# A decoder layer with attention, an S4D convolution and an expert stage: the convolution's transforms on folded halves, and new step lists

## The chip, the cores and the metric

The kernel runs on one core of one Trainium2 chip. Its time is the device time of an execution in microseconds (us); the number compared is the median of the runs. The engines are TensorE (PE; its weight loads are shown as PEld), VectorE (DVE), ScalarE (ACT), GpSimd (POOL) and SyncE (SP), which issues most of the DMAs.

## The reference

Input x is (4, 512, 128) in fp32; everything is fp32 with a norm behind each of three sublayers.

```python
x = layernorm(x + attention(x))        # 16 heads of 8, 4 kv heads, rms norm, rope, tanh cap 50, causal
x = layernorm(x + xattn(x, ctx_768))   # below
x = layernorm(x + ffn(x))              # 2 shared experts + top 2 of 8, hidden 512

def s4d(x):                            # inside xattn
    K  = 2 * real(einsum('dn,dnl->dl', dC, exp(dtA[:, :, None] * arange(L))))
    Kf = rfft(K, n=2 * L);  xf = rfft(x, n=2 * L, axis=1)
    return irfft(xf * Kf.T, n=2 * L, axis=1)[:, :L] + x * D_skip
# xattn: c = top-32 cross attention over 32 context rows; x = layernorm(x) * (1 + g*scale_in(c)) + g*shift_in(c)
#        y = s4d(x) * (1 + g*scale_out(c)) + g*shift_out(c); xt = x_text + y
#        xt = xt + gelu(layernorm(xt) @ W1 + b1) @ W2 + b2; return layernorm(xt)
```

## The kernel before

Every engine plays a list of steps written out in full (`PE_ORDER`, `ACT_ORDER`, `POOL_ORDER`, `DVE_ORDER`, played by `play`). A step name is followed by its numbers: `s.1.3.4` is batch 1, head pair 3, score fill 4. The order on an engine is exactly that of its list, and the engines meet at semaphores. SyncE has its own program, which issues loads and stores in order.

**Attention.** For each of 4 batches: `xT`, `qkv`, rms norm and rope (`squares`, `rms`, `rope`, `parts`, `copies`), `qT` (queries and keys transposed, six banks evacuated by ScalarE and VectorE in turn), then for 8 head pairs six score fills `s` into two PSUM banks `ring_s`; ScalarE evacuates each with tanh and then does one `exp` per pair; POOL masks; TensorE multiplies by the values (`PV`, one per two pairs), VectorE copies (`oT`). `probs` holds three pairs. Then `rows`, `yT`, `proj`, `x1`.

**The S4D kernel.** While batch 0 and the start of batch 1 run, VectorE, ScalarE and POOL compute exponentials and angles in four parts (`steps`, `states`, `pack`, then `angles`, `turns`, `exponents`, `powers`, `products`, `amounts` with .0 to .3), TensorE multiplies them (`taps`), VectorE writes `kij` (`evacuate`), which goes out to DRAM and comes back as `kld` (`load_kernel`). `first_tap` adds the skip. `kernel.0` to `kernel.7` transform it with the tables `cosm` and `sin_fwd`, and `spectra` scales the result into `kc`, `ks`, `kcn`.

**The convolution.** Per batch, xn is normed and modulated (`film`, `modulate`); `dft.b.0` to `.7` multiply xn (four tiles of 128 tokens) with `cosm` and `sin_fwd` (512 x 512, four row tiles) into `ring_u`; `spectrum` multiplies by the kernel's spectrum; `conv.b.0` to `.7` multiply back with `cosm` and `sin_inv` into `bank_d`; `shape_out` follows, then a feed-forward (`h`, `hT`, `up`, `gelu`, `down`, `ffT`, `ff_norm`, `x2_norm`, `x2`). Each of dft and conv has 8 x 4 products of 128 x 128 by 128 x 128.

**Start of the program.** `functions` (two sines and a tanh for the S4D states) and `fold1` to `fold4` (the cross attention's weights multiplied together) run at the head of the lists; `vf.b` on VectorE evacuates `fold4`.

**Experts.** `x2T`, `gates`, `route`, `weights`, `rank`, `place` per batch; for each group of two batches `rows.g` on VectorE builds the table of blocks (`table_ready`) and the row numbers (`rows_ready`). POOL scatters the tokens to DRAM (`scatter.b.j`, two issues each, 16 issues a group). SyncE waits for the scatters, loads the rows back in six loads (`load_rows`, `x_blk`) and then one 514 KB block of expert weights for each of 23 blocks of 128 rows (`load_block`, six slots). The units are numbered 0 to 77: 0 to 15 shared experts of batches 0 and 1, 16 to 38 the blocks of group 0, 39 to 54 shared experts of batches 2 and 3, 55 to 77 the blocks of group 1. A unit has `blk_up`, `blk_gelu` and `blk_down`; a block also has `blkT` (transpose of its rows, `xT_blk` with `RING` slots, copied by VectorE), `weigh` (VectorE, into `y_blk` with `YS` slots) and `blk_out` (POOL sends it to DRAM by indirect DMA). At the end SyncE loads the pairs back (`load_pair`), VectorE adds and norms (`pairs`, `out_begin`, `out_end`) and SyncE stores.

A y slot is free when its send has landed:

```python
def weigh(s):
    dve.wait_ge(u_down, s + 1)
    if k >= YS:
        dve.wait_ge(y_sent[k % YS], 16 * (k // YS))
```

## Time and profile before

| what | us |
|---|---|
| median of 3 runs (558.0 to 561.37) | 561.07 |
| the profiled execution | 563.88 |
| its span, first to last instruction | 562.1 |
| busy: TensorE / VectorE / ScalarE / POOL | 443.5 / 330.3 / 328.2 / 247.3 |
| granted TensorE clock, mean of the span | 0.904 |

The busy time of an engine is the sum of its instructions. A matmul is pipelined with the next, so the time of one is longer than the distance between two; the distance is what a stretch of them costs. The granted clock of 1.00 is 2.4 GHz, 0.50 is 1.2 GHz. "[2.28 <-DVE y_blk L1838]" behind a row says that the engine was idle for 2.28 us before it, until that instruction of VectorE released it. Terms of the plan are told from the profiled execution, whose span is 1.0 us above the median.

### The profile page before, as it was taken

The page shows a single profiled execution, that of the slowest core. Times are in us where ns is not written, and L with a number is a line of the kernel's source. Part 1 is how long each engine was busy: PE and PEld are TensorE (multiplying, and loading weights), DVE is VectorE, ACT ScalarE, POOL GpSimd, SP SyncE. Part 2 cuts the span into 40 slices and gives each one's busy share as a digit, 9 for nine tenths or more (in the row PEclk, how much of TensorE's full clock was granted, in tenths as well). Part 3 has the DMA queues.
Part 4 walks back from the last instruction along what each step waited for, and adds up shares of the span by engine and source line. Part 5 has one row for each costly group of instructions (what it writes and reads, how often), then busy time and mean ns, then how long its engine had stood idle before and what let it go on. Part 6 is the DMA issues. An engine that isn't in the chain of part 4 may idle for free.

```text
span 562.1 us, 9639 instructions
## 1 busy us (share of the span) xinstructions
PE 443.5 (79%) x3343; PEld 316.1 (56%) x3361; DVE 330.3 (59%) x983; ACT 328.2 (58%) x567; POOL 247.3 (44%) x306
## 2 busy tenths in 40 slices
PE   4656667378988879788798999999979699989830
PEld 3322323145657633567346865787778666878830
DVE  7877968847876565866754775546245310334214
ACT  4279769997775888877896152215536343445410
POOL 3513264423561565614446244864283574044341
PEclk9856656679999999999999999999998899999985
DMA  3788300002101000000000200165485516769831
GB/s 94 267 181 152 100 2 1 0 2 58 77 1 77 20 2 0 2 1 1 2 0 1 76 2 19 40 179 194 138 260 160 163 54 182 261 208 279 271 104 37
DMA packets 39920, 51.53 MB, mean 92 GB/s; under 512 B 8769, under 2 KB 29025, under 8 KB 39873
## 3 DMA queue, kind: packets, MB, share of 16 engines
q1 hardware_dynamic: 37376, 45.78, 28.1%
q0 software_dynamic: 2496, 5.15, 2.6%
q8 instruction: 27, 0.44, 0.3%
q14 instruction: 21, 0.16, 0.1%
HBM read 41.25 MB, written 13.86 MB: 98 GB/s over the span
## 4 chain that ended last, share of the span: by engine, by line
PE 47%; ACT 22%; DVE 9%; issue 8%; POOL 8%; DMA 5%; another core or an unknown queue 1%; POOLq 0%; SPq 0%; ACTq 0%; DVEq 0%
ACT probs L1082 8%; PE ring_s L957 5%; ACT probs L1088 5%; PE bank_o L987 4%; PE bank_o L775 4%; PE bank_d L865 3%; DMA token_pairs<-y_blk,x_blk 3%; PE ring_s L760 3%; PE bank_o L973 3%; PE ring_s L951 3%; POOL expert_rows L1302 3%; PE ring_u L852 3%; PE bank_d L894 2%; PE ring_u L844 2%; PE bank_r L641 2%
## 5 line engine op out<-in xcount | busy, mean ns | idle before, releaser
L1082 ACT ACTIVATE probs<-ring_s 128x512 f32<-128x512 f32 (+1 forms) x192 | 92.3, 524 | 39.2 <-PE ring_s L760 19.5
L760 PE MATMUL ring_s<-qT,kT 128*128 128x128 bf16 (+3 forms) x238 | 62.5, 330 | 41.6 <-ACT probs L1082 31.3
L1254 POOL TENSOR_SCALAR_AFFINE_SELECT probs<-probs 128x256 f32<-128x256 f32 (+1 forms) x96 | 50.6, 558 | 100.1 <-ACT probs L1088 100.1
L1135 ACT ACTIVATE g_ring<-ring_s,w_blk 128x128 f32<-128x128 f32 x184 | 52.3, 371 | 47.5 <-PE ring_s L957 47.5
L1088 ACT ACTIVATE probs<-probs 128x2560 f32<-128x2560 f32 x32 | 74.4, 2335 | 1.1
L1311 POOL DMA_INDIRECT token_pairs<-y_blk,x_blk x46 | 44.6, 970 | 66.2 <-DVE y_blk L1838 59.9
L760 PEld LDWEIGHTS ring_s<-qT,kT 128*128 128x128 bf16 x256 | 20.8, 100 | 80.2 <-ACT probs L1082 61.0
L957 PE MATMUL ring_s<-xT_blk,w_blk 128*128 128x128 f32 x368 | 51.1, 284 | 5.9 <-DVE xT_blk L1831 3.9
L1188 POOL TENSOR_TENSOR rstd<-var_eps,neg_half 128x4 f32<-128x4 f32 x24 | 25.0, 1040 | 67.4 <-DVE var_eps L1507 67.4
L957 PEld LDWEIGHTS ring_s<-xT_blk,w_blk 128*128 128x128 f32 x368 | 46.5, 198 | 7.9 <-ACT g_ring L1135 4.3
L775 PE MATMUL bank_o<-probs,vv 128*32 128x128 f32 (+3 forms) x512 | 43.2, 483 | 3.7 <-POOL probs L1254 3.6
L1131 ACT ACTIVATE g_ring<-ring_s,vcols 128x512 f32<-128x512 f32 x32 | 21.7, 687 | 40.8 <-PE ring_s L951 40.8
L987 PE MATMUL bank_o<-w_blk,g_ring 128*128 128x128 f32 x280 | 40.2, 290 | 4.1 <-DVE y_blk L1838 4.1
L1302 POOL DMA_INDIRECT expert_rows<-x_rows,rows_i x32 | 31.6, 989 | 20.5 <-DVE gmax L1823 11.6
L987 PEld LDWEIGHTS bank_o<-w_blk,g_ring 128*128 128x128 f32 x280 | 36.5, 203 | 6.1 <-issue 5.6
L973 PEld LDWEIGHTS bank_o<-w_sh,g_ring 128*128 128x128 f32 x256 | 32.9, 192 | 11.7 <-issue 11.7
L973 PE MATMUL bank_o<-w_sh,g_ring 128*128 128x128 f32 x256 | 33.8, 275 | 0.0
L951 PE MATMUL ring_s<-x2T,w_sh 128*128 128x512 f32 x64 | 32.8, 597 | 0.3 <-ACT g_ring L1131 0.3
L775 PEld LDWEIGHTS bank_o<-probs,vv 128*32 128x32 f32 x512 | 16.0, 119 | 30.2 <-issue 22.3
L1831 DVE COPY xT_blk<-bank_m 128x128 f32<-128x128 f32 x35 | 10.1, 287 | 34.0 <-PE bank_m L641 33.8
L1838 DVE TENSOR_SCALAR y_blk<-bank_o,x_blk 128x128 f32<-128x128 f32 x35 | 12.2, 348 | 27.8 <-PE bank_o L987 21.4
L747 PE MATMUL ring_s<-identb,qs 128*128 128x128 bf16 x128 | 11.8, 260 | 7.9 <-issue 3.5
(365 smaller groups left out, 932.3 us busy)
## 6 DMA issues: line engine op xcount, KB each, us to landing
w_blk<-expert_pack SPq DMA_DIRECT2D x46, 514.0 KB, 5.0
expert_pack<-in_L_ffn_W SPq DMA_DIRECT2D x16, 256.0 KB, 8.9
expert_rows<-blank SPq DMA_DIRECT2D x6, 520.0 KB, 3.6
x_blk<-expert_rows SPq DMA_DIRECT2D x10, 260.0 KB, 4.4
y_pair<-token_pairs SPq DMA_DIRECT2D x4, 512.0 KB, 4.9
x_in<-in_x SPq DMA_DIRECT2D x4, 256.0 KB, 2.9
cosm<-in_c_cos SPq DMA_DIRECT2D x1, 1024.0 KB, 5.9
sin_fwd<-in_c_sin_fwd SPq DMA_DIRECT2D x1, 1024.0 KB, 8.8
```

Of the source, the lines that this page charges most:

```text
L760: last = mm(bank[:, c:c + w], kT[:, r, p // 2, P * j:P * (j + 1)], qT[:, p, P * j:SEQ], start=True, stop=True)
L775: last = mm(bank_o[32 * h:32 * h + 32, P * j:SEQ], vv[:, j, q, :], probs[:, (2 * quad + h // 2) % PAIRS_HELD, c:c + SEQ - P * j], start=(j ...
L951: last = mm(bank[:, :], w_sh[:, e, P * n:P * (n + 1)], x2T[:, of, :], start=True, stop=True)
L957: last = mm(bank[:, P * n:P * (n + 1)], w_blk[:, k % SLOTS, P * n:P * (n + 1)], xT_blk[:, k % RING, :], start=True, stop=True)
L973: last = mm(bank_o[:, P * j:P * (j + 1)], g[:, P * j:P * (j + 1)], w_sh[:, e, HID + P * n:HID + P * (n + 1)], start=(c == 0 and j == 0), s ...
L987: last = mm(dst, g[:, P * n:P * (n + 1)], w_blk[:, k % SLOTS, HID + HC + P * n:HID + HC + P * (n + 1)], start=(n == 0), stop=(n == HC - 1))
L1082: f(probs[:, pair % PAIRS_HELD, BASE[n]:BASE[n] + WIDTH[n]], ring_s[k % 2][:, 0:WIDTH[n]], ACT.Tanh, scale=1.0 / (CAP * float(np.sqrt(np.f ...
L1088: f(probs[:, (b * NPAIR + p) % PAIRS_HELD, :], probs[:, (b * NPAIR + p) % PAIRS_HELD, :], ACT.Exp, scale=CAP).then_inc(exp_done, 1)
L1135: last = f(g_ring[:, s % RING, P * n:P * (n + 1)], ring_s[s % 2][:, P * n:P * (n + 1)], ACT.Gelu, bias=w_blk[:, k % SLOTS, HID + n:HID + n ...
L1254: last = g.affine_select(out=v, in_=v, compare_op=ALU.is_ge, fill=0.0, base=0, pattern=[[0, v.shape[1]], [1, P]], channel_multiplier=-1)
L1302: g.indirect_dma_start(out=rows_dram, out_offset=bass.IndirectOffsetOnAxis(ap=rows_i[:, k, j:j + 1], axis=0), in_=x_rows[:, k, j, :], in_o ...
L1311: g.indirect_dma_start(out=pair_dram, out_offset=bass.IndirectOffsetOnAxis(ap=x_blk[:, k % NB, D:D + 1].bitcast(I32), axis=0), in_=y_blk[: ...
```

## The change

Three things change together.

**Folded transforms.** The frequencies are moved by half a sample, so that the transforms of the even and of the odd half of a folded sequence need tables of half the size. `halves` (26 small VectorE instructions by Newton steps on 128 x 4 values) computes the cosines and sines of the half step, `half.0` to `.3` turn the loaded tables by it, and `tab.0` to `.3` transpose them on TensorE for the forward direction (ScalarE copies them out). The tables loaded are `cos_inv` and `sin_inv`, four loads of 256 KB, instead of three of 1 MB. `flip` is a matrix that turns a tile over, made by three POOL operations. `mirror` (two products with it) and `fold` (VectorE, two operations on 128 x 256) make sums and differences of xn and its mirror image; `dft` and `conv` then have 8 x 2 products each; `unfold` (three operations), `back` (two products) and `shape_out` in two parts undo it. The kernel goes the same way (`kmirror`, `kfold`, `kernel`), and `spectra` turns its spectrum by the half step.

**Experts.** `RING` goes from 3 to 4 and `YS` from 3 to 6. SyncE requests the first six weight blocks of a group as soon as `table_ready` comes, ahead of its wait for the scatters; for group 1 it also waits for the sent blocks of group 0 and loads the first pair of batches before that wait. The load of x for batch 2 goes ahead of the kernel's way through DRAM.

**Lists.** All four lists are written anew, with the new steps in them. `taps` uses `ring_u` instead of `bank_d` and `bank_r`.

```diff
-RING = 3
+RING = 4
 SLOTS = 6
-YS = 3
+YS = 6
@@ PE_ORDER, the start (before, then after)
-    xT.0 qkv.0 fold1 fold2 fold3 fold4 vectors qT.0.0 qT.0.1 qT.0.2 qT.0.3 qT.0.4 s.0.0.0 s.0.0.1 s.0.0.2 s.0.0.3
+    xT.0 qkv.0 qT.0.0 qT.0.1 qT.0.2 fold1 qT.0.3 qT.0.4 qT.0.5 fold2 fold3 fold4 s.0.0.0 s.0.0.1 s.0.0.2 s.0.0.3
...
+    s.0.2.4 s.0.2.5 s.0.3.0 PV.0 s.0.3.1 s.0.3.2 xT.1 s.0.3.3 s.0.3.4 s.0.3.5 rows.0 qkv.1 PV.1 taps.0 s.0.4.0
...
@@ PE_ORDER, around gates.3 (before, then after)
-    blk_down.26 blkT.30 blk_up.29 x2T.3 blk_down.27 blkT.31 gates.3 blk_up.30 blk_down.28 blkT.32 blk_up.31
+    blk_down.24 hT.3 blkT.28 blk_up.27 up.3.0 up.3.1 up.3.2 up.3.3 down.3.0 down.3.1 down.3.2 down.3.3 blk_down.25
+    blk_up.35 x2T.3 blk_down.33 blkT.37 blk_up.36 blk_down.34 blkT.38 gates.3 blk_up.37 blk_down.35 blk_up.38
+    blk_down.36 rank.3 blk_up.39 blk_down.37 blk_up.40 blk_down.38 blk_up.41 blk_down.39 blk_up.42 blk_down.40
...
+    blk_up.53 blk_down.51 blkT.55 blk_up.54 blk_down.52 blkT.56 blk_up.55 blk_down.53 blkT.57 blk_up.56 blk_down.54
@@ ACT_ORDER, the start (before, then after)
-    xT.0 qkv.0 functions fold1 fold2 fold3 qT.0.0 qT.0.2 qT.0.4 s.0.0.0 s.0.0.1 s.0.0.2 s.0.0.3 s.0.0.4 s.0.0.5
+    xT.0 qkv.0 qT.0.0 qT.0.2 functions fold1 fold2 fold3 qT.0.4 s.0.0.0 s.0.0.1 s.0.0.2 s.0.0.3 s.0.0.4 s.0.0.5
@@ POOL_ORDER, the scatters (after)
+    mask.3.6 mask.3.7 root copies.1 root root shape_out.2 copies.0 root h.2 xn.3 scatter.1.0 scatter.1.1 scatter.1.2
+    blk_out.34 blk_out.35 blk_out.36 scatter.3.0 blk_out.37 blk_out.38 scatter.3.1 scatter.3.2 scatter.3.3
@@ DVE_ORDER, the start (before, then after) and around rows.1 (after)
-    steps squares.0 rms.0 rope.0 parts.0 v.0 copies.0 vectors vf.0 qT.0.1 vf.1 qT.0.3 states pack angles.0 turns.0
+    steps squares.0 rms.0 rope.0 parts.0 copies.0 halves qT.0.1 qT.0.3 half.0 half.1 vf.0 vf.1 qT.0.5 v.0 states pack
+    vectors angles.0 turns.0 oT.0 vf.2 vf.3 half.2 half.3 products.0 amounts.0 angles.1 evacuate.0 turns.1 tokens.0
+    gates.3 route.3 weigh.35 weights.3 weigh.36 place.3 rows.1 weigh.37 weigh.38 settle.46 blkT.55 blkT.56 blkT.57
@@ SyncE
+            for m, k in ((cos_inv, "c_cos"), (sin_inv, "c_sin_inv")):
+                rows = t[k].rearrange("(h p two) f -> two p h f", h=NJ, two=2)
+                for odd in range(2):
+                    load(m[:, NJ * odd:NJ * (odd + 1), :], rows[odd][:, :, 0:HALF], ld_dft)
...
             for g in range(GROUPS):
                 sp.wait_ge(table_ready, g + 1)
+                for q in range(SLOTS):
+                    load_block(g * NB + q)
+                if g:
+                    sent(g - 1)
+                    load_pair(GB * (g - 1))
                 sp.wait_ge(scattered[g], 16 * 2 * NT * GB)
                 for n in range(x_loads):
                     load_rows(g, n)
+                if g:
+                    load_pair(GB * g - 1)
+                for q in range(SLOTS, NB):
@@ TensorE
+            def turn_over(dst, src, at):
+                for j in range(NJ):
+                    last = mm(dst[:, P * j:P * (j + 1)], flip[:, :], src[:, at + NJ - 1 - j, :], start=True, stop=True)
+                return last
+            def half_dft(f, c, src):
+                at = 0 if (f == 0) == (c < NJ) else NJ
+                for j in range(NJ):
+                    last = mm(ring_u[f][:, P * c:P * (c + 1)], (cos_fwd, sin_fwd)[f][:, j, P * c:P * (c + 1)], src[:, at + j, :],
+                              start=(j == 0), stop=(j == NJ - 1))
+                return last
             def dft(b, n):
                 f, c = divmod(n, NT)
                 if n == 0:
-                    pe.wait_ge(xmod_ready, b + 1)
-                mat = (cosm, sin_fwd)[f]
-                for j in range(NT):
-                    last = mm(ring_u[f][:, P * c:P * (c + 1)], mat[:, j, P * c:P * (c + 1)], xn[:, j, :],
-                              start=(j == 0), stop=(j == NT - 1))
+                    pe.wait_ge(fold_ready, b + 1)
+                last = half_dft(f, c, xn)
...
@@ VectorE
+            def half(c):
+                then()
+                if c:
+                    dve.wait_ge(half_ready, c)
+                co, si = cos_inv[:, c, :], sin_inv[:, c, :]
+                op(ts(turned[0][:, :], si, sin_b[:, c:c + 1], None, ALU.mult))
+                one(ts(turned[1][:, :], co, sin_b[:, c:c + 1], None, ALU.mult))
+                op(stt(out=co, in0=co, scalar=cos_b[:, c:c + 1], in1=turned[0][:, :], op0=ALU.mult, op1=ALU.subtract))
+                stt(out=si, in0=si, scalar=cos_b[:, c:c + 1], in1=turned[1][:, :], op0=ALU.mult, op1=ALU.add).then_inc(half_ready, 1)
+            def fold_over(x, ps):
+                one(tt(x[:, NJ:NT, :], x[:, 0:NJ, :], ps, ALU.subtract))
+                return tt(x[:, 0:NJ, :], x[:, 0:NJ, :], ps, ALU.add)
...
```

## Rows read from the trace of the kernel before

**Rows 1.** Stages: busy us (x) of PE, PEld, DVE, ACT, POOL; clock, DMA.

```profile
33.70:111.80 78.10, 46.45 (x361) 20.76 (x364) 63.53 (x120) 66.27 (x87) 31.77 (x39) 0.61 0.35 71
111.80:174.60 62.80, 53.65 (x547) 35.72 (x551) 43.94 (x115) 50.99 (x70) 25.40 (x40) 0.94 0.13 42
174.60:246.30 71.70, 61.28 (x489) 38.93 (x496) 49.95 (x143) 55.50 (x76) 34.90 (x46) 1.00 0.03 10
246.30:311.00 64.70, 55.01 (x425) 35.61 (x426) 40.30 (x117) 48.97 (x68) 28.10 (x39) 1.00 0.00 1
311.00:378.00 67.00, 65.50 (x425) 49.49 (x414) 40.75 (x148) 19.48 (x28) 35.05 (x33) 1.00 0.20 58
...
482.70:539.40 56.70, 50.29 (x421) 47.27 (x420) 21.09 (x77) 27.05 (x94) 22.59 (x24) 1.00 0.70 225
```

**Rows 2.** TensorE's groups by line: records, busy us, mean ns, idle before.

```profile
L865 PE MATMUL bank_d<-spec,cosm 128*128 128x128 f32 x128 | 17.2, 278 | 0.1
...
L852 PE MATMUL ring_u<-xn,cosm 128*128 128x128 f32 x128 | 16.9, 279 | 0.1
...
L705 PE MATMUL ring_u<-pv,cosm 128*128 128x128 f32 x32 | 4.1, 275 | 0.1
```

**Rows 3.** The chain in order of time: start us, us, what.

```profile
187.63 3.57 PE bank_d L865 x32
```

**Rows 4.** VectorE's groups by line and shape, three widths.

```profile
L1838 DVE TENSOR_SCALAR y_blk<-bank_o,x_blk 128x128 f32<-128x128 f32 x35 | 12.2, 348 | 27.8 <-PE bank_o L987 21.4 <-DMA token_pairs<-y_blk,x_blk 6.4
...
L1507 DVE TENSOR_SCALAR var_eps<-mean_var 128x4 f32<-128x4 f32 x24 | 4.1, 171 | 0.8
...
L1703 DVE TENSOR_TENSOR spec<-spec,fb 128x512 f32<-128x512 f32 x4 | 2.8, 692 | 0.1
```

**Rows 5.** Timeline of ScalarE, 9 to 27: start us, us, instruction, [idle before].

```profile
9.21 1.28 ACT L1006 ACT_TABLE_LOAD   x1
...
26.39 1.02 ACT L1071 ACTIVATE qT<-ring_s 128x1024 bf16<-128x1024 bf16 x1 [8.53 <-PE ring_s L747]
```

**Rows 6.** Timelines of SyncE and VectorE, 16 to 26.

```profile
16.52 0.51 SPq L503 DMA_DIRECT2D sin_inv<-in_c_sin_inv  x1
...
24.75 0.43 DVE L1590 COPY k_parts<-k_parts 128x1024 bf16<-128x1024 bf16 x1
```

**Rows 7.** DMA issues by line: count, KB each, median us to landing.

```profile
x_blk<-expert_rows SPq DMA_DIRECT2D x10, 260.0 KB, 4.4
...
sin_inv<-in_c_sin_inv SPq DMA_DIRECT2D x1, 1024.0 KB, 10.8
```

**Rows 8.** Timelines of POOL, SyncE, TensorE at group 0's rows.

```profile
345.17 1.23 POOL L1302 DMA_INDIRECT expert_rows<-x_rows,rows_i  x1 [6.52 <-DVE gmax L1823]
...
370.93 3.29 SPq L503 DMA_DIRECT2D x_blk<-expert_rows  x6
...
378.01 0.27 PE L641 MATMUL bank_m<-ident,x_blk 128*128 128x128 f32 x1
```

**Rows 9.** Timelines of VectorE and TensorE at a y slot's wait.

```profile
419.99 0.35 DVE L1838 TENSOR_SCALAR y_blk<-bank_o,x_blk 128x128 f32<-128x128 f32 x1 [2.40 <-DMA token_pairs<-y_blk,x_blk]
...
420.49 2.05 PE L987 MATMUL bank_o<-w_blk,g_ring 128*128 128x128 f32 x8 [2.28 <-DVE y_blk L1838]
```

**Rows 10.** Timelines of TensorE, POOL, SyncE from hT.3 to group 1.

```profile
391.20 0.60 PE L641 MATMUL bank_r<-ident,fa 128*128 128x128 f32 x4
...
426.85 0.96 PE L913 MATMUL bank_r<-router_w,x2T 128*128 128x8 f32 x8
...
439.62 0.96 POOL L1302 DMA_INDIRECT expert_rows<-x_rows,rows_i  x1 [5.06 <-DVE gmax L1823]
...
469.92 0.96 POOL L1302 DMA_INDIRECT expert_rows<-x_rows,rows_i  x1 [0.30 <-issue]
...
472.73 3.23 SPq L503 DMA_DIRECT2D x_blk<-expert_rows  x6
...
482.75 0.27 PE L641 MATMUL bank_m<-ident,x_blk 128*128 128x128 f32 x1
```

399 lines of the change are left out of this document (240 added, 159 removed).

## The prediction

> **What bounds the kernel now.** I read the page's busy shares, then the busy time of each engine stage by stage, then the timelines of the places where an engine waits. The attention of the four batches ends near 311 us, the expert stage near 539, and 23 us of output follow. In batch 0 (33.7 to 111.8) ScalarE is busy 66.3 of 78.1 us and VectorE 63.5, because VectorE also builds the S4D kernel; TensorE has the lower clock there (0.61 granted), but is busy only 46 us. In batches 1 to 3 TensorE is the fullest engine, 53.7 of 62.8, 61.3 of 71.7 and 55.0 of 64.7 us, with ScalarE at 51.0, 55.5 and 49.0. From 311 to 378 TensorE is busy 65.5 of 67.0 [rows 1]. Later it is dense except for a few stalls. So a vector microsecond is dear before 112, a tensor microsecond is worth part of itself in batches 1 to 3, and nearly all of itself behind 311.
>
> **The transforms.** The fp32 product is two records: a batch has 64 products in `dft` and `conv` and the trace 128 records (L852 and L865 have 256 each, of which one of the two like groups stands here, and L705 64) [rows 2]. 32 records follow each other in 3.57 us, 0.112 us each [rows 3]. After the change a batch has 2 + 16 + 16 + 2 = 36 products, 72 records. It saves 56 x 0.112 = 6.3 us per batch. The S4D kernel's transform goes from 64 records to 36, -3.1 us, and the 16 transposes of `table` (one record each) add 1.8 us, up to 4 at the lower clock. In all 576 records become 324 + 16: 26 us less for TensorE. By place: batch 1 has half of a batch's transforms, the kernel's and 8 transposes: -3.1 - 3.1 + 1.1 = -5.1. Batches 2 and 3 have a batch's worth each, -6.3. Behind 311 lie conv.2, dft.3 and conv.3: -3.1 - 6.3 = -9.4.
>
> How much of the 17.7 us in batches 1 to 3 shortens them? TensorE is busy 85% of the time and ScalarE 77 to 81%, so another engine comes next soon. Bounds: nothing, and all 17.7. I take somewhat over half, **-10 us**.
>
> **What VectorE gets.** `halves` is 26 instructions on 128 x 4 elements. The row of that width is 171 ns, and with the hand-over by semaphore I take 0.2: 5.0 us. For the 256-wide operations the trace has no row; the bounds are 0.35 (128 x 128) and 0.69 (128 x 512) [rows 4]; I take 0.4. `half` x4 is 16 of them, 6.4 us; `fold`, `unfold` and the split `shape_out` add 2.3 us per batch. `spectra` becomes 16 instructions of 128 x 128 and a copy for 3 of 0.69: +4 us. In batches 1 to 3 VectorE has 35% free, so I cost these at nothing; without that cover they are 3 to 7 us per batch. In batch 0 it has 14.6 us free in 78, and 11 us are added.
>
> **The start.** The new lists put `halves` ahead of qT.0.1 and move `functions`, fold1, fold2 and fold3 on ScalarE behind qT.0.2, though ScalarE did all that from 9.2 to 17.9 and then was idle 8.5 us until the first transposed queries at 26.4 [rows 5]. The copies before it end near 25.1 [rows 6]; `halves` ends at 30.1 and qT.0.1 leaves its bank at 30.8. ScalarE does qT.0.2 by 29.6, then 3.3 us of functions and 0.6 us of fold1. TensorE has fold2 behind qT.0.5 (34), and its chain through kbd, wvf, xq and fold4 is most of that 8.7 us stretch of ScalarE's, 8 us, so to 42; qT.0.5 waits on VectorE for vf.0 and vf.1, which wait for fold4, and leaves its bank near 43. The first tanh of the scores opened the stage at 33.7 and comes near 42 to 43: **+9 us**. Behind it `states`, `pack`, `angles` and `turns` shift by 13, and taps.0 now stands ahead of s.0.4.0, so that scores wait for products. The new lists also mix tanh and exp of batch 0 anew, which can win some back. I take **+10 us** at the start of batch 1; bounds +3 (the lists win back most) and +22 (none won back, the 11 added vector microseconds all on the path). The tables must have landed by 25.1: three megabytes went out and the last, issued at 16.5, landed 10.8 us later, at 27.3 [rows 6, 7]; now one megabyte in four parts goes out, and at that pace it is there by 22. Flip's three small POOL operations stand ahead of the masks that fold1 needs, and fold1 now has time until 28: nothing. Four table copies on ScalarE are 0.6 us each: in the +10.
>
> So attention ends at 311 + 10 - 10 = 311.
>
> **The first expert group.** The rows of group 0 were loaded at 370.9 and TensorE took the first at 378.0 [rows 8]. TensorE's work now brings it there 9.4 us sooner, 368.6. POOL issues one scatter in 1.26 us (25 issues from 439.6 to 469.9 [rows 10]). The 16 of group 0 began at 345.2 [rows 8] and were mixed with norms; in the new list they stand together, 20.2 us, and 1.9 us (469.9 + 1.0 to 472.7) to the load makes 367.3, landing 4.4 us later at 371.7 (the median of such a load [rows 7]). So I take 371.8: -6.2. Six weight blocks are requested at `table_ready`, ahead of the scatters. Without that the weights would land 5 to 6 us behind the rows and eat most of the -6.2; they are what lets it stand. Then YS 3 to 6 removes a wait: VectorE stood 2.4 us for a sent y slot at 417.6 to 420.0, TensorE behind it 2.3 us, and then it ran at the lower clock: from 420.5 to 426.9 it did 30 records, 3.4 us at their spacing, in 6.4, so 3.0 are lost: -5.3 in all [rows 9, 10].  A stall on VectorE's `rows.1`, which stood ahead of row copies, goes too: the new list has all 23 row copies before it. It lies behind gates.3, where the chain counts, and is worth nothing in the sum.
>
> **The hand-over to group 1.** This is where that gain is given back. gates.3 moves from behind blk_up.30 to behind blkT.38, six units (12 us) later in TensorE's order; its data come by way of hT.3, ffT.3 and x2.3. A unit is 17 records, 1.9 us, so hT.3, now behind blk_up.26, is at 371.8 + 12 x 1.9 + 1.2 = 396 (391.2 before), and from there to gates.3 went 35.7 us with the 5.3 of stall in them, so it runs near 428 (426.9 before) [rows 10]. From it: 12.8 us to the first scatter (as before), 18 POOL issues at 1.26 us (16 scatters and blk_out.37 and .38; before they were mixed with nine) 22.7, 1.9 to the load, 4.4 to landing: 42, so blkT.55 near 470. TensorE has only 17 units and two biases, 31 us, ahead of it and stands about 11 us, near 459 to 470. Before: 482.75. That is **-12.7 us** for everything from 311 to blkT.55. The early weights count here as well: before, they were requested behind the six row loads, which take 3.2 us to issue [rows 10]; in that order they would add 4 to 5 us.
>
> **Group 1 and the end.** From 482.7 to 539.4 TensorE was busy 50.3 of 56.7 [rows 1]. The stalls there (y slots, row copies, one wait for a root on POOL) go in half by RING and YS: -3, and 1 us back since it starts at the lower clock: -2. The last sends no longer queue behind a blocked y copy: one issue, -1.3.
>
> **Sum.** +10 - 10 - 12.7 - 2 - 1.3 = -16 on the profiled span of 562.1: 546. That execution took 563.9 us with what lies around the span, the median of the three runs is 561.1; I take the median as the span less 1: **545 us**.
>
> **Rivals.** (a) VectorE becomes the bound of batch 0. For: 63.5 of 78.1 busy, 11 added, with `halves` ahead of everything and `rms.1`, `parts.1` behind the angles. Against: 14.6 us are free. Its price is the upper bound, +22 at batch 1, and with VectorE late the tensor saving of batch 1 is lost too (-5 instead of -10). The tail is counted from the end of attention, so 562 + 22 - 5 - 16 = 563, less 1, and with no gain in group 1 about 566; at +28 it is over 1% slower, near 570. It decides from a shift of batch 1 by 19 us. Chance 0.17, of which 0.1 slower.
> (b) Tensor time in batches 1 to 3 is not the bound (ScalarE's 51 to 56 us and its waits are). Then -10 becomes -2, 553. For: ScalarE and TensorE wait for each other in turn at two score banks. Chance 0.2.
> (c) The hand-over is longer than 42 us (POOL shares with blk_outs, gates.3 comes later than 428): 10 us more, 555 to 556. For: in the trace POOL and VectorE are in order and POOL's norms are on the way to x2.3. Chance 0.13.
> (d) The clock. In batch 0 the granted clock was 0.61 at 59% busy, in batch 1 0.94 at 85%, then 1.00 [rows 1]: the level of 1.2 GHz goes with waits between products. With 6 us less work per batch, batches 1 to 3 are 77% busy, and the 11 us stand before blkT.55 is a gap of a kind that at 417 to 420 did bring the lower level. If a third of each batch runs at it, some 15 us of products take twice their time, half of it on the path: +8 per batch, 545 + 24 = 569. Chance 0.08. The Trainium skill, "TensorE: Matmul & The Clock Gate", section "HAM oscillation — how this bites in real kernels", says that idle gaps between products send the engine back to the lower rate and each burst then starts cold. By that rule taking work away speaks against this change; the trace agrees at 420.5, and batches 2 and 3 at 1.00 with waits in them speak against its reaching so far.
> (e) The new order wins the whole front back and the stall at 459 is half: 545 - 7 - 5 = 533. Chance 0.1.
>
> My own forecast (540 to 551) has 0.32. The range: 532 to 567 leaves out part of (a), (d) and (e). Within 1% is 555.5 to 566.7, about what a measurement can tell from no change. Faster by over 1%: 0.32 + 0.2 + 0.07 of (c) + 0.1 = 0.69. Same: 0.07 of (a), 0.06 of (c), 0.02 of (d): 0.15. Slower: 0.16.
>
> **What would show it.** First tanh of the scores at 42 to 43, batch 1 near 121 (111 before). Records of L705, L852 and L865's successors 324 and no more. Attention's end (last PV) near 311; TensorE busy 78% in batches 2 and 3. First x_blk transpose near 372, gates.3 near 428, a TensorE stall of about 11 us ahead of blkT.55, named as row loads. No VectorE wait for sent y slots. I am wrong if batch 1 starts beyond 130, if batches 1 to 3 are as long as before, or if the stall ahead of blkT.55 is over 20 us.

## The result, and the profile after

| | before | after | forecast |
|---|---|---|---|
| median, us (5 runs each) | 560.73 (558.0 to 561.37) | 570.85 (568.43 to 574.2) | 545 |
| ratio to before | 1 | 1.0191 [1.0145, 1.0237] | |
| span of the profiled execution | 562.1 | 572.4 | 546 |
| first tanh of the scores | 33.7 | 43.0 | 42 to 43 |
| first tanh of batches 1, 2, 3 | 110.5, 180.7, 246.3 | 127.5, 198.1, 270.1 | batch 1 near 121 |
| last product with the values (end of attention) | 311.3 | 334.8 | 311 |
| first `x_blk` transpose | 378.0 | 397.3 | 371.8 |
| gates.3 | 426.8 | 454.4 | 428 |
| blkT.55 | 482.7 | 493.6 | 470 |
| last `weigh` | 539.0 | 549.7 | |

The rows behind the ratio are read from the profiled executions, of which that of the kernel after was the longest of its five (574.2 us). Ratios and their 95% intervals leave out executions more than 1.5% above the fastest of their kernel.

The changed kernel is 1.9% slower. Two more comparisons, each on another chip, gave 1.0237 [1.0186, 1.0288] and 1.0198 [1.0143, 1.0254]. The whole loss is there at the end of attention: +23.5 us where I forecast 0. From there to blkT.55 it wins 12.7 us (171.5 before, 158.8 after; I forecast -12.7), and behind that 0.5.

The table of busy time by stage of the kernel after, with the cuts of [rows 1] as far as they go (us from and to, length; busy us and records of PE, PEld, DVE, ACT, POOL; granted clock, DMA share, GB/s):

```profile
33.70:111.80 78.10, 48.16 (x284) 19.72 (x283) 57.09 (x132) 59.21 (x81) 33.36 (x45) 0.68 0.29 57
111.80:174.60 62.80, 43.22 (x469) 24.77 (x466) 45.49 (x110) 50.45 (x71) 22.13 (x30) 0.77 0.10 31
174.60:246.30 71.70, 56.48 (x392) 32.47 (x393) 49.10 (x134) 51.41 (x71) 29.31 (x41) 0.95 0.05 19
246.30:311.00 64.70, 52.09 (x403) 30.33 (x402) 44.49 (x140) 51.74 (x72) 28.47 (x38) 0.97 0.01 1
```

Beside [rows 1] the first stage holds less work: ScalarE 59.2 us for 66.3, VectorE 57.1 for 63.5, TensorE 284 records for 361. The work has not grown there, it comes later. TensorE did get less to do:

```profile
L915 PE MATMUL bank_d<-spec,cos_inv 128*128 128x128 f32 x64 | 10.0, 278 | 0.1
L739 PE MATMUL ring_u<-xn,cos_fwd 128*128 128x128 f32 x64 | 8.1, 277 | 0.1
L733 PE MATMUL ring_u<-xn,flip 128*128 128x128 f32 x16 | 2.6, 284 | 0.0
```

These are three of TensorE's groups by line. L865 and L852 had 128 records each [rows 2]. With the like groups (`sin_inv`, `sin_fwd`, the kernel's and the flips of `bank_d`) there are 324, as forecast, and 16 transposes of tables. The saving was there. What it was worth is the question of the experiments.

### The profile page after: what moved, and what is told of

Same layout as the page of the kernel before. It is cut to its first block, busy times and chain, and to the rows that moved or that the text cites. A ratio compares the mean times of both kernels' runs of the same rounds, so it can differ in the third digit from the quotient of the medians.

```text
span 572.4 us, 9281 instructions
## 1 busy us (share of the span) xinstructions
PE 428.2 (75%) x3125; PEld 288.0 (50%) x3125; DVE 347.5 (61%) x1065; ACT 332.2 (58%) x571; POOL 249.3 (44%) x309
## 4 chain that ended last, share of the span: by engine, by line
PE 43%; ACT 20%; DVE 13%; issue 10%; POOL 8%; DMA 4%; POOLq 0%; SPq 0%; ACTq 0%; DVEq 0%
ACT probs L1141 8%; PE ring_s L1011 6%; PE bank_o L823 5%; ACT probs L1147 4%; PE ring_s L808 3%; PE bank_o L1041 3%; PE ring_u L892 2%; PE bank_o L1027 2%; POOL expert_rows L1361 2%; POOL probs L1313 2%; DMA token_pairs<-y_blk,x_blk 2%; PE bank_d L915 2%; PE bank_m L662 2%; PE bank_d L948 2%; PE ring_s L1005 2%
## 5 line engine op out<-in xcount | busy, mean ns | idle before, releaser
L808 PE MATMUL ring_s<-qT,kT 128*128 128x512 bf16 (+3 forms) x256 | 69.5, 339 | 40.7 <-ACT probs L1141 31.8
L808 PEld LDWEIGHTS ring_s<-qT,kT 128*128 128x128 bf16 x256 | 21.4, 102 | 84.2 <-ACT probs L1141 68.3
L823 PE MATMUL bank_o<-probs,vv 128*32 128x128 f32 (+3 forms) x512 | 47.2, 519 | 6.7 <-POOL probs L1313 6.7
L1011 PE MATMUL ring_s<-xT_blk,w_blk 128*128 128x128 f32 x368 | 49.3, 277 | 3.0 <-DVE xT_blk L1968 1.7
L1011 PEld LDWEIGHTS ring_s<-xT_blk,w_blk 128*128 128x128 f32 x368 | 44.8, 192 | 4.7 <-ACT g_ring L1194 4.0
L1041 PE MATMUL bank_o<-w_blk,g_ring 128*128 128x128 f32 x280 | 38.0, 279 | 5.9 <-DVE y_blk L1975 5.9
L1027 PEld LDWEIGHTS bank_o<-w_sh,g_ring 128*128 128x128 f32 x256 | 33.1, 192 | 12.7 <-issue 12.7
L1041 PEld LDWEIGHTS bank_o<-w_blk,g_ring 128*128 128x128 f32 x280 | 34.2, 192 | 8.3 <-issue 6.7
L823 PEld LDWEIGHTS bank_o<-probs,vv 128*32 128x32 f32 x512 | 17.3, 125 | 35.8 <-issue 25.1
L795 PEld LDWEIGHTS ring_s<-identb,qs 128*128 128x128 bf16 x128 | 9.5, 114 | 26.3 <-issue 19.5
```

The costliest lines, as they stand in the source:

```text
L808: last = mm(bank[:, c:c + w], kT[:, r, p // 2, P * j:P * (j + 1)], qT[:, p, P * j:SEQ], start=True, stop=True)
L823: last = mm(bank_o[32 * h:32 * h + 32, P * j:SEQ], vv[:, j, q, :], probs[:, (2 * quad + h // 2) % PAIRS_HELD, c:c + SEQ - P * j], start=(j ...
L1011: last = mm(bank[:, P * n:P * (n + 1)], w_blk[:, k % SLOTS, P * n:P * (n + 1)], xT_blk[:, k % RING, :], start=True, stop=True)
L1027: last = mm(bank_o[:, P * j:P * (j + 1)], g[:, P * j:P * (j + 1)], w_sh[:, e, HID + P * n:HID + P * (n + 1)], start=(c == 0 and j == 0), s ...
L1041: last = mm(dst, g[:, P * n:P * (n + 1)], w_blk[:, k % SLOTS, HID + HC + P * n:HID + HC + P * (n + 1)], start=(n == 0), stop=(n == HC - 1))
```

## The experiments

Kernels measured together ran on one chip and share the runs of the kernel before there. The kernel before took 559 to 561 us on some chips and 571 to 580 on others; the last section tells what differs in the traces. So totals are compared on one chip only. Up to the end of attention the chips agree: kernels with the lists of before end it at 309.8 to 314.2 on all of them.

### Is it the head of the lists?

The first suspicion was `halves` and the late `fold` steps at the start. `a_head` is the kernel after with this part of its lists put back nearly as before, and `a_head2` is the same kernel on another chip.

```diff
 PE_ORDER
-xT.0 qkv.0 qT.0.0 qT.0.1 qT.0.2 fold1 qT.0.3 qT.0.4 qT.0.5 fold2 fold3 fold4 s.0.0.0
+xT.0 qkv.0 fold1 fold2 fold3 fold4 vectors qT.0.0 qT.0.1 qT.0.2 qT.0.3 qT.0.4 qT.0.5 s.0.0.0
 DVE_ORDER
-copies.0 halves qT.0.1 qT.0.3 half.0 half.1 vf.0 vf.1 qT.0.5 v.0 states pack vectors angles.0 turns.0
+v.0 copies.0 vectors vf.0 qT.0.1 vf.1 qT.0.3 qT.0.5 states pack angles.0 turns.0 halves half.0 half.1
```

> The changed kernel with the head of its lists put back: functions, fold1 to fold3 on ScalarE and fold1 to fold4 and vectors on TensorE stand ahead of qT.0.0 again; on VectorE the halves and half.0, half.1 go behind turns.0 and half.2, half.3 behind vf.3, and qT.0.5 stands ahead of states. Theory O (the order of the lists is what costs): the first tanh of the scores comes at 34 instead of 43, the 9 us stay to the end, and the kernel takes 562 to 565. Rival V (the added vector work makes VectorE the bound of batch 0): the first tanh comes early as well, but the 11 us of added vector work are still there, batch 1 opens no sooner than 124, and the time stays within 3 us of the changed kernel, 568 to 571. Rival C (the lower clock in batches 0 and 1 sets the pace): a gain of at most half of the 9 us, 566 to 568.

> The kernel of a_head once more, since TensorE's semaphore increments came late behind 360 us there. Theory O: the first tanh at 33, batch 1 at 117 to 120, attention's end at 321 to 326, as there; and with increments on time the total is 561 to 565.

Measured: first tanh at 32.3 and 33.7 (41.1 to 43.0 in three traces of the kernel after), but batch 1 at 119.3 and 122.4 (125.4 to 127.5), and attention ends at 325.5 and 330.4 (330.1 to 334.8). Ratios 1.0432 [1.0359, 1.0505] and 1.0458 [1.0399, 1.0517], on chips of the slower kind. Of some 9 us won at the head 3 to 8 are left at batch 1, where theory O wanted all of them to the end. The head costs what I forecast, but it is not the main cause.

### Is it VectorE's new work, or the order?

`a_nohalf` is the kernel after without the work on the half-sample tables: `halves` sets two small tiles to constants and `half` does one tiny memset, so the tables aren't turned. `a_head_nohalf` is the same with the head of `a_head`.

```diff
 def half(c):
-    co, si = cos_inv[:, c, :], sin_inv[:, c, :]
-    op(ts(turned[0][:, :], si, sin_b[:, c:c + 1], None, ALU.mult))
...
+    v.memset(turned[0][:, 0:1], 0.0).then_inc(half_ready, 1)
```

> The changed kernel without the work that makes the half-sample tables on VectorE: the 24 small instructions that find the half-angle columns and the 16 instructions of half.0 to half.3 (128 x 256) are left out, two memsets and four tiny ones stand for them (the tables are then not shifted by half a sample). All lists are as changed. Rival V (the added vector work is what lengthens the start and batch 0, 5.0 + 6.4 us by my prices): first tanh 4 us sooner, batch 1 opens at 116 to 120 instead of 126, total 561 to 565. Theory O (the order of the lists, not the work in it): first tanh and batch 1 within 2 us of the changed kernel, total 568 to 572.

> The changed kernel with the head of its lists put back as in a_head, and without the half-sample table work on VectorE as in a_nohalf (tables not shifted by half a sample). With the head put back, batch 1 opened 3 to 6 us sooner, not 9, and VectorE was busy 74 of batch 0's 88.7 us; with the table work left out but the head as changed, nothing moved. If the two stand in each other's way (the changed order hides the 10 us of table work ahead of the late first tanh, and the repaired head brings them into batch 0, where VectorE is full): first tanh at 33, batch 1 at 114 to 117, attention's end at 319 to 323. If the table work costs nothing anywhere: batch 1 at 119 to 122, attention's end at 326 to 330.

Measured: `a_nohalf` has its first tanh at 40.9 and batch 1 at 125.7, the kernel after 41.3 and 125.6 in its second execution. In the stage from the one to the other:

```profile
41.00:125.80 84.80, 51.01 (x398) 23.09 (x398) 62.96 (x138) 67.33 (x88) 33.51 (x38) 0.63 0.19 38
```

VectorE is busy 63.0 us for 65.9 and nothing is shorter. `a_head_nohalf` has 34.1 and 119.1, `a_head` and `a_head2` 32.3 and 119.3, 33.7 and 122.4. So the table work costs nothing in the changed order, and 0 to 3 us at batch 1 behind the mended head; that the two stand in each other's way, my next idea, fell (114 to 117 was forecast). The rest of the new work of VectorE (`fold`, `unfold`, `spectra`) was left out in neither.

The other half of the question is `b_neworder`: the kernel before, products and all, with the lists of the kernel after less the new steps (`tab`, `kmirror`, `mirror`, `back`, `halves`, `half`, `kfold`, `fold`, `unfold`), `RING` 4, `YS` 6 and the early weights. It ran beside `a_head`.

```diff
-RING = 3
+RING = 4
-YS = 3
+YS = 6
 PE_ORDER
-... hT.0 up.0.0 up.0.1 s.2.4.3 s.2.4.4 up.0.2 s.2.4.5 s.2.5.0 up.0.3 PV.9 s.2.5.1 down.0.0 down.0.1 down.0.2 down.0.3 s.2.5.2
+... s.2.5.3 s.2.5.4 up.0.1 up.0.2 up.0.3 film.1.0 film.1.1 film.1.2 down.0.0 down.0.1 down.0.2 s.2.5.5 s.2.6.0 s.2.6.1
...
```

> The kernel before with its own full transforms (no halves, no folds, none of the added vector work), but with the new lists in all four engines (the new steps taken out), RING 4, YS 6 and the early weights. Theory O: batch 1 opens at 124 or later, attention ends at 335 or later although no vector work was added, and with the full transforms the kernel is slower than the changed one: 575 to 590. Rival V: without the added vector work batch 1 opens at 116 or sooner, attention ends near 320 and the time is 560 to 567.

Measured: 623.54 us, 1.0924 [1.084, 1.1008]. Attention ends at 348.0; `b_loads` (below), which has the old lists and the same slots and loads, ends it at 311.3 on the same chip. Theory O is borne out, and its 575 to 590 was too low. Here are the four batches of the kernel before in a second execution, of the kernel after in a second execution, and of `b_neworder`. The cuts were set by hand near the first tanh of each batch, up to 1.5 us from it:

```profile
32.60:109.30 76.70, 46.90 (x360) 20.63 (x360) 62.37 (x118) 65.22 (x86) 31.63 (x38) 0.61 0.37 75
109.30:176.30 67.00, 58.66 (x613) 38.03 (x614) 48.30 (x123) 53.59 (x74) 26.29 (x41) 0.96 0.13 45
176.30:245.40 69.10, 59.90 (x443) 37.69 (x440) 46.65 (x138) 53.83 (x75) 34.90 (x46) 0.98 0.02 5
245.40:310.30 64.90, 56.01 (x428) 35.72 (x427) 40.46 (x120) 48.56 (x68) 28.12 (x39) 1.00 0.00 1
```

```profile
41.30:125.70 84.40, 48.79 (x398) 20.88 (x398) 65.86 (x144) 67.35 (x88) 33.54 (x38) 0.67 0.16 36
125.70:195.00 69.30, 53.15 (x511) 32.14 (x512) 53.36 (x138) 54.88 (x77) 25.98 (x39) 0.88 0.09 28
195.00:265.50 70.50, 54.34 (x365) 30.24 (x364) 45.22 (x135) 54.05 (x75) 31.95 (x42) 0.98 0.05 20
265.50:330.20 64.70, 54.55 (x408) 31.01 (x406) 45.30 (x143) 49.17 (x68) 30.96 (x44) 0.97 0.00 1
```

```profile
41.10:125.70 84.60, 46.39 (x386) 19.61 (x385) 64.05 (x133) 66.45 (x86) 32.26 (x38) 0.65 0.25 48
125.70:199.20 73.50, 60.68 (x565) 38.51 (x564) 48.51 (x120) 53.96 (x75) 26.62 (x39) 0.85 0.09 26
199.20:278.00 78.80, 63.62 (x416) 38.11 (x416) 42.92 (x135) 54.53 (x75) 33.41 (x46) 0.91 0.05 18
278.00:348.80 70.80, 62.19 (x465) 38.77 (x463) 40.60 (x125) 48.58 (x67) 28.52 (x39) 0.93 0.01 1
```

By the exact first tanh of each batch and the last product with the values the lengths are:

| | head | batch 0 | batches 1, 2, 3 | their sum |
|---|---|---|---|---|
| old order, old transforms | 32.3 | 76.6 | 68.8, 67.2, 65.0 | 201.0 |
| new order, new transforms | 41.3 | 84.4 | 69.3, 70.5, 64.6 | 204.4 |
| new order, old transforms (`b_neworder`) | 40.3 | 84.5 | 73.6, 78.7, 70.8 | 223.1 |

The order of the lists costs 8.1 at the head, 7.9 in batch 0 and 22.1 in batches 1 to 3, together 38.1 us (36.7 against `b_loads`); the smaller transforms, with all that came with them, give 18.7 of it back. The other traces of the kernel before have 200.7 for the sum, those of the kernel after 207.4 and 207.6, so what is given back is 15.5 to 18.7. ScalarE's work is the same in all three (221.2, 225.5 and 223.5 us in attention). What grew is the time in which it is not busy, by the windows above: in batches 1 to 3 45.0 us in the old order, 66.0 in the new one with the old transforms, 46.4 with the new ones; in batch 0 11.5, 18.2 and 17.1. That is nearly the whole cost of the order.

One site can be read off. In the new `PE_ORDER` nine products of 512 columns in fp32 stand between two score fills: s.2.5.4, up.0.1 to up.0.3, film.1.0 to film.1.2, down.0.0 to down.0.2, s.2.5.5. ScalarE's timeline there, first of the kernel after, then of `b_neworder` (start us, us, instruction, idle before it and who ended it):

```profile
244.27 2.82 ACT L1141 ACTIVATE probs<-ring_s 128x256 f32<-128x256 f32 x6 [5.11 <-PE ring_s L808]
```

```profile
254.63 2.82 ACT L1091 ACTIVATE probs<-ring_s 128x256 f32<-128x256 f32 x6 [5.11 <-PE ring_s L769]
```

Both stand 5.11 us until the next fill. The longest wait of ScalarE for a fill in the kernel before was 3.4 us, in its waits:

```profile
ACT probs L1082 <- PE ring_s L760: 30.2, 44, 3.4
```

The length of the run alone does not make the wait. Before, eight such products and two columns of `dft` stood between s.3.6.3 and s.3.6.4, and in the new lists ten stand between s.3.6.1 and s.3.6.2. There ScalarE had `gelu`, `exp` and `ff_out` to do meanwhile, and waited 1.45 us in the kernel before and 0.96 in `b_neworder`:

```profile
295.53 0.38 ACT L1082 ACTIVATE probs<-ring_s 128x256 f32<-128x256 f32 x1 [1.45 <-PE ring_s L760]
```

```profile
331.04 1.08 ACT L1091 ACTIVATE probs<-ring_s 128x512 f32<-128x512 f32 x2 [0.96 <-PE ring_s L769]
```

At s.2.5.5 it had nothing else. A second wait of this size is not for a fill: at attnT.1, a transpose of the cross attention that stands behind PV.9 and rows.8 on TensorE, ScalarE waits 5.06 us in `b_neworder` and 4.97 in the kernel after; before, its waits for this bank in batch 2 add up to 1.4. (The step writes the tile `x1T`.)

```profile
237.25 0.60 ACT L1112 ACTIVATE x1T<-bank_r 128x512 f32<-128x512 f32 x1 [5.06 <-PE bank_r L650]
```

No other single wait for a fill is over 3 us in the new order; the rest of the 22.1 is spread over many places, and none was tried by itself.

For batch 0 VectorE's waits from the first tanh to batch 1 tell the places (waiting line, releaser: us in total, times, longest), of the kernel before and then of the kernel after:

```profile
DVE pv L1479 <- ACT ue L1044: 2.0, 2, 1.4
```

```profile
DVE pt L1530 <- ACT pv L1093: 6.7, 1, 6.7
DVE pv L1544 <- ACT ue L1103: 4.5, 2, 2.6
DVE uf L1536 <- ACT ug L1089: 3.2, 1, 3.2
```

The S4D kernel's pieces go to and fro between ScalarE and VectorE. VectorE stood 14.4 us for them in the new order and 2.0 in the old; in `b_neworder`, without any new step, these waits are 16.6. This fits the 7.9 us, but I did not mend these places one by one, so it is a reading. What lengthens batch 0 to 85 to 89 us when the head is mended stays open.

### What is a microsecond of TensorE worth in attention?

`b_half` is the kernel before with half the products of `dft`, `conv` and `kernel`; the sums are incomplete. Nothing else moves.

```diff
-for j in range(NT):
+for j in range(NT // 2):
     last = mm(ring_u[f][:, P * c:P * (c + 1)], mat[:, j, P * c:P * (c + 1)], xn[:, j, :], ...)
```

> The kernel before with nothing changed but that dft, conv and the kernel's transform leave out every second half of their products (32 instead of 64 records' worth in each batch; the sums are then incomplete): TensorE gets what the change gives it and more (32 products fewer per batch, 7.2 us, and 3.6 once), and no engine gets any new work. It measures by itself the step that I took at -10 us for batches 1 to 3 (by its size here 7.2 + 7.2 + 7.2 = 21.6 us less, of which I would have counted 12) and the 10.8 us behind attention. Theory O (TensorE's time inside attention is worth little, since each score fill waits for ScalarE): attention ends at 303 to 308, total 550 to 556. My forecast's step: attention ends at 299 or sooner, total 545 or less. Rival C (less work brings the lower clock, which eats the gain): attention ends at 309 or later with a granted clock under 0.97 in batches 2 and 3, total 556 or more.

Measured: 559.19 for 559.46, 1.0005 [0.9964, 1.0046]. Up to the end of attention the trace has 193 transform records for 385, 21.5 us less of TensorE at the 0.112 us of [rows 3], and attention ends at 309.9 for 309.9. Its batches 1 to 3:

```profile
110.70:177.90 67.20, 55.11 (x552) 32.23 (x552) 49.67 (x127) 53.70 (x75) 25.88 (x40) 0.94 0.13 45
177.90:243.90 66.00, 54.19 (x373) 31.50 (x372) 45.09 (x134) 53.59 (x75) 34.88 (x46) 0.95 0.02 5
243.90:310.20 66.30, 53.54 (x362) 30.88 (x362) 40.45 (x122) 48.37 (x68) 29.85 (x40) 0.90 0.00 1
```

By the exact first tanhs they take 67.3 + 66.0 + 66.5 = 199.7 us, 1.3 less than before. Batch 3 with 65 fewer records is 1.5 us longer: the granted clock is 0.90 where it was 1.00, and 7.3 us less work lowered the busy time by 2.5. In batch 2 the clock took less (between its exact first tanhs 60 records, 6.7 us, went and the busy time fell by 4.6), and still only 1.3 us were won. So both theory O and rival C have a part, and every sign that I had set for rival C came true; this run cannot part them further. In the old order these products, the clock that they hold up included, are worth next to nothing.

`a_double` is the kernel after with the products of `dft` and `kernel` done twice and the conv columns filled with as many extra products, so TensorE has somewhat over the old amount of transforms in the new order (412 records in batches 1 to 3; 385 before, 220 after).

```diff
-for j in range(NJ):
+for j in [*range(NJ)] * 2:
     last = mm(ring_u[f][:, P * c:P * (c + 1)], (cos_fwd, sin_fwd)[f][:, j, P * c:P * (c + 1)], ...)
```

> The changed kernel with every product of dft and kernel issued twice and four extra products in each column of conv (results unchanged): TensorE's products are back at the number before, all else is as changed. Theory O and no part of the clock: attention gets 8 to 14 us longer (335 to 343 or more) and the kernel 15 to 25 us longer, 585 to 595. Rival C (the lower clock of batches 1 to 3 is what lost the gain): the granted clock rises from 0.77 in batch 1 and 0.95 in batch 2, attention ends at 338 or sooner and the kernel takes 575 to 583.

> The changed kernel once more, beside the others. Where the late increments are absent: 570, attention ends at 335, ratio 1.02. Where they are there: 585 to 600, since its sixteen scatters of a group stand together, with the same front.

Measured on the chip of `b_half`: `a_double` 601.08, 1.0778 [1.0702, 1.0855]; the kernel after 571.46. Attention ends at 344.4 for 330.1. Its batch 0 is 84.8 us, its batches 1 to 3 are 77.0 + 74.3 + 68.3 = 219.5, 15.1 above the 204.4 of the kernel after, for 192 records, 21.5 us. `b_neworder` has 164 records more than the kernel after in these batches, 18.4 us, and is 18.7 us longer. So the same products are worth next to nothing in the old order and most or all of their time in the new one. That this is because scores wait in line behind runs of other products fits ScalarE's idle time above; it was not tested by moving single products.

> The kernel before once more, for its trace on the same chip as the runs beside it. In the four experiments before this, semaphore increments of TensorE were seen 1 to 16 us late while POOL's indirect DMAs landed (none was late by over 1 us in the first traces of the kernel before and of the changed one), and the kernel before took 566 to 579 us there instead of 561. If that belongs to the chip, this trace shows it for all four kernels of this call or for none; attention ends at 311 in either case, since no indirect DMA runs before that.

The kernel before gave 557.88 there, with increments on time and the end of attention at 309.9, and its trace is the one used for comparison above.

### Do the smaller transforms pay in the old order?

`a_oldfront` is the kernel after, with the lists of before up to the end of attention and the new steps put in at places that I chose: on TensorE tab.0 and tab.1 behind s.0.6.2, mirror.0 behind s.1.7.3, back.0 behind x1T.1, and so on. Against the list of before:

```diff
 PE_ORDER
-... s.0.6.2 ... s.1.7.3 ... s.1.7.5 ... x1T.1 ...
+... s.0.6.2 tab.0 tab.1 ... s.1.7.3 mirror.0 ... s.1.7.5 dft.0.0 dft.0.1 dft.0.2 ... x1T.1 back.0 ...
```

> The changed kernel with the whole order of the kernel before up to the end of attention (the new steps put where their data are ready), and with its own new order behind it. Theory O: batch 1 opens at 110 to 114, attention ends at 311 to 317, from there the stretch is as in the changed kernel (13 us shorter than before), and the time is 553 to 558. It also shows what the smaller transforms are worth inside attention: if attention ends at 311 they are worth nothing there, at 301 what I had forecast. Rival V: VectorE carries the same added work, batch 1 opens at 122 or later and the time is 565 to 571.

Measured: 603.17, 1.0564 [1.0485, 1.0643], attention ends at 338.8, far beyond either theory. Its trace is of its longest execution (609.43; the other three took 599.55 to 603.31). There the first tanh is at 33.5 and batch 1 at 116.1, the best start of all versions with the new steps, but batches 1 to 3 take 75.9, 71.7 and 75.2, as long as the new order with the old transforms. VectorE is busy 72.1 of the 82.6 us of batch 0. In batch 3 TensorE stands 3.1 us until VectorE has folded xn, with a score fill in line behind it, and ScalarE waits 6.5 us for that fill. So the new steps are not free in every order. The gain was not to be had by my placement; it is one placement, not the best, and whether the smaller transforms pay in any order stays open.

### What do the expert part's changes bring?

`b_loads` is the kernel before with the slots and SyncE's order of after, `b_slots` has the slots alone (the first four lines), `b_tail` is `b_loads` with the lists of after behind attention.

```diff
-RING = 3
+RING = 4
-YS = 3
+YS = 6
 SyncE
+                for q in range(SLOTS):
+                    load_block(g * NB + q)
                 sp.wait_ge(scattered[g], 16 * 2 * NT * GB)
```

> The kernel before, with its own transforms and its own four lists, and with only RING 4, YS 6 and the early weights with the new order of SyncE's loads. Expected, if the gain behind attention is that of the slots and of the early weights: attention ends at 311 as before, blkT.55 comes 4 to 12 us sooner, and the time is 549 to 556. Rival: the gain behind attention comes from the smaller transforms there (9.4 us less for TensorE); then this kernel takes 558 to 561.

> The kernel of b_loads once more for the same reason: the kernel before with only RING 4, YS 6 and the early weights in SyncE's new order. Expected with increments on time: attention ends at 311, blkT.55 at 470 to 478, total 549 to 555. If the gain behind attention belongs to the smaller transforms alone: 558 to 561.

> The kernel before with only RING 3 to 4 and YS 3 to 6 (more slots for hidden rows and for weighted blocks), the order of SyncE's loads as before. My prediction gave the y-slot stall 5.3 us on the way to blkT.55 and 2 us in group 1. If that holds, with the rest of before: 553 to 556. If the stall is only moved (blkT.55 waits for its rows, not for TensorE): 558 to 561. Measured against the kernel before on the same chip: ratio 0.988 to 0.992 or 0.998 to 1.002.

> The kernel of b_loads again, on a chip of which I hope that TensorE's increments are on time. With the early weights and the slots of the change and everything else as before: the first x_blk transpose is where it was (377, rows and weights come from the same point), blkT.55 4 to 6 us sooner, total 549 to 555, ratio 0.983 to 0.990. If the early weights and slots are worth nothing without the new lists: 0.998 or more.

> The kernel before, own transforms and own lists up to the end of attention; behind that the new lists (the new steps taken out), RING 4, YS 6, early weights. Beside b_loads3 it shows what the new order behind attention is worth by itself. If the new order there is what gained 9 us up to blkT.55: blkT.55 at 468 or sooner and total 549 or less. If the gain is the slots' and the early weights': as b_loads3 within 2 us. If the new order, in which gates.3 stands six blocks later, costs when TensorE has the full transforms: 3 to 6 us above b_loads3.

| | ratio | blkT.55 | chip |
|---|---|---|---|
| `b_loads` | 1.0035 [0.9982, 1.0087] | 493.7 | before takes 574 |
| `b_loads2` | 0.9966 [0.9919, 1.0013] | 492.7 | 572 |
| `b_loads3` | 0.998 [0.9942, 1.0019] | 494.0 | 580 |
| `b_slots` | 0.9989 [0.9957, 1.0022] | 499.5 | 580 |
| `b_tail` | 1.0231 [1.0159, 1.0303] | 506.4 | 580 |

None can be told from the kernel before but `b_tail`, which is slower, by more than any of its three forecasts. All five ran on chips of the slower kind (below). A last set ran on one of the other kind.

> The kernel before with the slots and the early weights only. With increments on time: 549 to 555, ratio 0.983 to 0.990, if slots and early weights gain without the new lists; 0.998 or more if they do not. With late increments it has given 1.0035, 0.9966 and 0.998, and gives 0.995 to 1.003 again.

> The changed kernel itself. With increments on time: ratio 1.019 to 1.024 as twice before. With late increments: the front is the same (batch 1 at 126, attention's end 330 to 335), behind it the sixteen scatters in a row and the late increments cost more than they cost the kernel before, ratio 1.03 to 1.05.

> The kernel before, for its trace beside the next two. If TensorE's increments come late on this chip: attention ends at 311 to 315, blkT.55 at 490 to 500 instead of 477 to 483, total 570 to 580. If not: as before_again, 556 to 562.

Measured: before 559.37, after 571.07, and slots with early weights 558.6 over 12 runs, 0.9945 [0.9908, 0.9982]. Slots and early weights alone are about 3 us faster than the kernel before on this chip, half of the least gain that was forecast, and the three sets before could not tell them apart. The trace does not show where: VectorE has no wait for a sent y slot, but from the end of attention to blkT.55 it takes 167.1 us, the kernel before there 166.2 and after 158.7. So the new tail's 7.5 to 12.7 us do not come from slots and early weights alone, nor from smaller transforms alone (`b_half` 168.2, `before_again` 167.2). What is left is the new order of the expert part, or the parts together; that is not shown, since the new order without the transforms was only tried where increments came late, and lost there.

## Why the prediction was wrong, by its own steps

**The step that failed: the order inside attention was never priced.** I worked out what moved at the head, behind attention and at the hand-over. Of batch 0 I wrote that scores wait for taps.0 and that the new mixing of tanh and exp "can win some back", and of the order in batches 1 to 3 nothing; their only term was the -10 of the smaller transforms. With the transforms of before, the order costs 7.9 us in batch 0 and 22.1 in batches 1 to 3 (`b_neworder`). My sum had no term for the 22.1, and none of the rivals named it. Of my own signs of being wrong, one came true: batches 1 to 3 were not shorter but 6.6 us longer (207.4 for 200.8 in the first traces).

**The start, +10.** The head was right: first tanh 43.0 for 42 to 43. The prices were near: `halves` ran from 24.0 to 28.4, 4.4 us for 5.0. A 256-wide operation is 0.35 to 0.60 in the mean by the rows after, for 0.4. But `halves` was not what held the head up: without it the first tanh still comes at 40.9 (`a_nohalf`) and 40.3 (`b_neworder`), so nearly all of the 9 us comes with the other moves in the lists, such as those of the functions and folds, and the right number had in part the wrong reason. ScalarE's timeline of the kernel after, four rows from the first queries to the scores:

```profile
25.34 1.02 ACT L1130 ACTIVATE qT<-ring_s 128x1024 bf16<-128x1024 bf16 x1 [16.18 <-PE ring_s L795]
...
33.09 1.11 ACT L1075 ACTIVATE kbd<-ring_u 32x128 f32<-32x128 f32 x4 [0.64 <-PE ring_u L685]
...
36.02 0.60 ACT L1083 ACTIVATE xq<-bank_d 128x512 f32<-128x512 f32 x1 [1.21 <-PE bank_d L690]
...
42.98 5.85 ACT L1141 ACTIVATE probs<-ring_s 128x512 f32<-128x512 f32 x12 [4.43 <-PE ring_s L808]
```

ScalarE stood idle 16.2 us, the time in which it did the functions and folds before [rows 5], and then did them ahead of the scores. But batch 1 began 16.9 us later, not 10: the head's 9.3 and the order of batch 0.

**The transforms in attention, -10.** Mis-sized both ways, by what the share of busy time can't tell. In the old order these products are worth 1.3 us of 21.5 (`b_half`); in the new one 15.5 to 18.7 us, most or all of my 17.7. "TensorE is busy 85%" [rows 1] was true and no evidence that less work shortens the stage.

**Behind attention, -12.7.** The sum was right, 158.8 us for 171.5, and part of that is luck. My 171.5 came from the longest of three traces of the kernel before; the others have 167.2 and 166.2, and all three of the kernel after 158.4 to 158.8, so chip by chip the gain is 12.7, 8.8 and 7.5. "Nearly all of itself behind 311" was not so for a tensor microsecond: `b_half` has the first `x_blk` transpose 4.4 us sooner, but blkT.55 no sooner. By parts errors cancel: the first `x_blk` transpose comes 4.2 us sooner after attention's end, I had 6.2; gates.3 57.0 us after it, I had 56; gates.3 to blkT.55 39.2, I had 42. The 16 scatters of group 1 stand nearly together, the first and the last at:

```profile
466.52 0.96 POOL L1361 DMA_INDIRECT expert_rows<-x_rows,rows_i  x1 [5.05 <-DVE gmax L1960]
...
488.01 0.96 POOL L1361 DMA_INDIRECT expert_rows<-x_rows,rows_i  x1 [0.30 <-issue]
```

Before, they took from 439.6 to 469.9 [rows 10]. Two things inside came out otherwise. The stall ahead of blkT.55 was 2.1 us, not 11; TensorE had spent part of the gap in another stall at 466, where `weigh.37` stands behind place.3 and rows.1 on VectorE. I had counted rows.1's stall as gone. And a wait for sent y slots was left, 4.5 us in three of them.

```profile
466.17 1.13 PE L1041 MATMUL bank_o<-w_blk,g_ring 128*128 128x128 f32 x8 [3.19 <-DVE y_blk L1975]
...
493.56 0.33 PE L662 MATMUL bank_m<-ident,x_blk 128*128 128x128 f32 x1 [2.08 <-DMA x_blk<-expert_rows]
```

```profile
DVE y_blk L1975 <- DMA token_pairs<-y_blk,x_blk: 4.5, 3, 1.8
```

The third execution of the kernel before has 8.6 us in eight such waits, and the version with slots and early weights alone gains 3 us on the whole. The -5.3 that I put on the y slot was read off one stall [rows 9]. With `b_slots` at 0.9989 [0.9957, 1.0022], if only on a chip of the slower kind, it was too much.

**Group 1 and the end, -3.3.** It was -0.5.

**The rivals.** (a) VectorE as the bound of batch 0 comes near in size at batch 1 (a shift of 16.9; it was to decide from 19) and has the wrong cause: without the table work nothing changes (`a_nohalf`). (b) was right for the old order and wrong for the new one. (c) did not happen, 39.2 for 42. (d) The clock fell where I said it could, in part: 0.88 in batch 1 for 0.96, then 0.98 and 0.97. It is not the whole loss: `a_double` reached 1.00 in batches 2 and 3 and took 142.6 us for them, with 2.6 us more of transforms, where the kernel before took 132.2 at 0.98 and 1.00. It can be a part of it: `b_neworder`, at 0.91 and 0.93 there, took 149.6. How much of the 22.1 is the clock was not measured by itself. `b_half` shows the effect by itself, 0.90 in batch 3 with fewer products and nothing else changed. The rule of the Trainium skill, "TensorE: Matmul & The Clock Gate", section "HAM oscillation — how this bites in real kernels", that idle gaps send the engine back to the lower rate, agrees with that row; it did not decide the sign of the result. (e) asked for the front to be won back, and the reverse happened.

## What to carry to other kernels

When a diff rewrites the lists, compare them step by step at the scarcest hand-over, here the two score banks: count how much foreign work of TensorE stands between two fills, and price each run against the work that ScalarE has in hand at that place; nine products cost 5.1 us where it had none, ten cost 1.0 where it had some. Do not count less work on the fullest engine as a gain until a kernel with half of that work is measured; here an 85% busy engine that waits in turn with a second one at 80% gave 1.3 us for 21.5 us less. And keep parts of a change apart: the two constants and the early weights gave 0.5% by themselves on one chip, while the lists they came with cost 38 us in attention.
